# Loading and scaling the mixer's weights inside the convolution, bias per item on VectorE in its last pass, and the first taps loaded apart

## The chip, the cores and the metric

The kernel runs on one core of a Trainium2 chip. The time is device microseconds of one launch. A core has TensorE (PE) for matmuls, with results in PSUM, VectorE (DVE), ScalarE (ACT), GpSimd (POOL) and SyncE (SP), which here only issues transfers. Each engine works through its own instructions in order; semaphores tie them together.

## What is computed

Two layers on x, 64 images of 55 x 55 pixels and 96 channels, f32. The convolution is depthwise: every channel has 25 x 25 taps of which every third row and column counts, without the middle one.

```
m[ix_(arange(0, 25, 3), arange(0, 25, 3))] = 1;  m[12, 12] = 0
lat = depthwise_conv(x, raw_kernel * m, padding='SAME')
x1  = lat * x + bias + x
t   = tokens(x1)                                     # 3025 tokens of 96 per image
h   = relu(bn1(ln(t) @ w1.T));  X = fft(h, over the tokens)
y   = real(ifft(relu(Re(X)*rd - Im(X)*id + rb) + 1j*relu(Im(X)*rd + Re(X)*id + ib)))
t   = t + bn2(y @ w2.T)
out = t + qlinear(relu(qlinear(ln(t), W1, b1)), W2, b2)   # products in 5-bit-exponent, 2-bit-mantissa floats
```

The batch norms' scales and shifts are folded into w1 and w2 on the chip: that is the scaling of the weights, with 1 / sqrt(var + eps) from a Sqrt on ScalarE, a reciprocal and one Newton step on VectorE.

## The kernel before

`build` calls `conv_stage` and then `mixer_stage`; each ends its instruction blocks with all engines meeting.

**The convolution** (L181 to L355) runs 16 passes t: for each of 8 groups of 12 channels (e = t // 2) first the image rows of kind 0, then of kind 1 (k = t % 2). A pass has 36 items n: a channel (n // 3) and a column phase (n % 3). On TensorE an item is three matmuls of x blocks with the channel's band of taps (`toep`, L351) and three transposes of the same blocks by the unit matrix (`unit`, L354), into a pair of PSUM banks; there are four pairs (DEEP = 4), and item m waits until item m - 4 is gated. ScalarE copies the transposed x into `xo` (L297), VectorE then makes (lat + 1) * x there (L328, "the gate"). When all 36 items of a pass are gated, GpSimd adds the bias over the whole pass (`add_bias`, L306): three instructions of 128x3960 for kind 0, two of 128x3300 for kind 1. Of the last pass the second one is VectorE's (`on_dve`). SyncE loads the taps of the next channels, x groups (6 items each) into a ring of three, and stores finished parts of `xo`; a store waits for its part's bias. Before its first matmul TensorE waits for `unit`, then for all 12 channels' taps, then for the first x group. ScalarE's queue issues cbias (the bias on all partitions, 128x96) and then `unit` (114x114), the others are SyncE's.

**The mixer** starts with a block of its own for the weights (L419 to L600): 37 loads (L459), among them the tables fb and ib of the transform (1.8 MB together); VectorE's scaling in steps that wait for each other through w_step (L506 to L558); ScalarE's Sqrt (L575); 36 small matmuls that turn the weights (L584 to L593), and memsets of the mixer's buffers (L563 to L569). After it SyncE issues the first two token loads (L727). The main block then runs over slots g, in which each engine's work for several chunks of tokens stands in a fixed order; VectorE's statistics of the tokens (L1015) and their scaling on GpSimd (L789) come first. In that loop the lines L944 to L960 are the layer norm's root, L969 and L975 the bias and rounding of the feed-forward part, L775 and L779 GpSimd's last additions.

What makes TensorE wait for a gate, and how deep it may run ahead:

```
if m >= DEEP:
    pe.wait_ge(gated, m - DEEP + 1)
```

## Time and profile before

| | |
|---|---|
| three runs, median (lowest, highest) | 4963.41 us (4961.54, 4970.19) |
| profiled execution | 4956.23 us |
| its span, first to last instruction | 4954.4 us |
| mean granted TensorE clock | 0.958 of full |
| busy PE, DVE, ACT, POOL | 4493.3, 3606.6, 3658.7, 2290.2 us |
| DMA | 895.69 MB, mean 181 GB/s |

The profile is of one execution, and the times in it are of that one. Busy time counts an engine's own instructions, not its waits or the issuing of transfers. A row of the timeline has the start, the duration, the engine, the line and operation, the tiles and shapes, how many such instructions follow each other (x), and in brackets how long the engine had been idle and what it waited for last. "SPq" and "ACTq" are the queues of issued transfers.

### The profile page before, as it was taken

To read this page: it belongs to the slowest core of one execution; us is meant where nothing else is said; L and a number is where in the kernel's file an instruction comes from. 1 tells how busy PE (TensorE), PEld (TensorE's weight loads), DVE (VectorE), ACT (ScalarE), POOL (GpSimd) and SP (SyncE) were. 2 spreads that over 40 slices of the span, in tenths; PEclk is the share of its full clock that TensorE was granted. 3 is DMA by queue.
4 is the path that set the end of the run, shared out by engine and by line. 5 is a ranking of instruction groups with operands and counts; after the bars stand their busy time and mean duration, and the time that the engine had idled before them with its cause. 6 is when DMAs were issued, how large, how long until landed. Compare 5 with 4: busy or idle time off the path is not lost.

```text
span 4954.4 us, 170251 instructions
## 1 busy us (share of the span) xinstructions
PE 4493.3 (91%) x64799; PEld 3661.4 (74%) x64799; DVE 3606.6 (73%) x10875; ACT 3658.7 (74%) x7819; POOL 2290.2 (46%) x2603
## 2 busy tenths in 40 slices
PE   8999995699999999999999999999999999999964
PEld 7888885477777777777777777777777777777742
DVE  3444443247888888888888888888888888888865
ACT  3444442377888888888888888888888888888843
POOL 2334432144554545555455555555555555455532
PEclk9999997599999999999999999999999999999975
DMA  6877876366666666666667666666666666666541
GB/s 199 253 235 231 257 227 177 81 173 184 185 182 177 185 176 186 181 185 181 178 179 190 181 185 186 182 186 177 181 179 183 184 182 185 177 180 190 162 102 31
DMA packets 787259, 895.69 MB, mean 181 GB/s; under 512 B 241827, under 2 KB 694880, under 8 KB 774368
## 3 DMA queue, kind: packets, MB, share of 16 engines
q1 hardware_dynamic: 786200, 884.70, 64.1%
q8 instruction: 534, 8.75, 0.8%
q14 instruction: 261, 2.14, 0.1%
q10 hardware_dynamic: 264, 0.10, 0.0%
HBM read 500.05 MB, written 384.61 MB: 179 GB/s over the span
## 4 chain that ended last, share of the span: by engine, by line
PE 57%; DVE 12%; ACT 8%; issue 5%; DMA 0%; DVEq 0%; POOL 0%; POOLq 0%; ACTq 0%
PE ps L1102 13%; PE ps L1089 10%; ACT y L886 7%; PE ps L1121 7%; PE ps L1197 5%; PE ps L1130 4%; PE ps L1146 4%; PE ps L1186 4%; PE ps L1160 4%; PE ps L1173 3%; PE ps L1076 2%; DVE y L969 1%; DVE bn L1022 1%; DVE xn L1007 1%; DVE var L946 1%
## 5 line engine op out<-in xcount | busy, mean ns | idle before, releaser
L763 POOL TENSOR_SCALAR gv<-gv 128x400 f32<-128x400 f32 (+1 forms) x512 | 488.6, 954 | 1673.1 <-DVE xn L1007 1445.3
L1102 PE MATMUL ps<-hid,fa 121*128 121x384 f32 (+1 forms) x2048 | 808.6, 477 | 42.9 <-DVE t L1031 30.6
L351 PE MATMUL cps<-toep,xin 114*128 114x190 f32 (+2 forms) x3456 | 773.1, 338 | 38.7 <-issue 19.8
L886 ACT ACTIVATE y<-ps 128x1089 f16<-128x1089 f32 (+1 forms) x512 | 572.9, 1119 | 314.5 <-PE ps L1186 314.5
L1089 PE MATMUL ps<-w1t,xnt 97*121 97x192 f32 x3200 | 708.9, 332 | 4.8 <-issue 4.2
L297 ACT ACTIVATE xo<-cps 128x180 f32<-128x180 f32 (+3 forms) x576 | 367.6, 638 | 442.4 <-PE cps L354 442.4
L328 DVE SCALAR_TENSOR_TENSOR xo<-cps,xo 128x180 f32<-128x180 f32 (+3 forms) x576 | 362.8, 630 | 450.8 <-ACT xo L297 450.1
L351 PEld LDWEIGHTS cps<-toep,xin 114*128 114x128 f32 x3456 | 529.2, 193 | 102.0 <-issue 25.0
L975 DVE CAST hq<-y 128x1092 fp8e5<-128x1092 f16 (+1 forms) x512 | 537.0, 1049 | 53.1 <-DVE y L969 0.5
L840 ACT ACTIVATE hid<-ps 121x384 f32<-121x384 f32 (+1 forms) x1024 | 438.0, 428 | 174.2 <-PE ps L1089 174.0
L969 DVE TENSOR_SCALAR y<-y,b1q 128x364 f16<-128x364 f16 (+1 forms) x1536 | 476.0, 365 | 107.9 <-ACT y L886 107.9
L306 POOL TENSOR_TENSOR xo<-xo,conv_cbias 128x3960 f32<-128x3960 f32 (+1 forms) x39 | 317.7, 8175 | 506.0 <-DVE xo L328 506.0
L1089 PEld LDWEIGHTS ps<-w1t,xnt 97*121 97x121 f32 x3200 | 530.7, 189 | 23.7 <-issue 5.9
L990 DVE SCALAR_TENSOR_TENSOR spec<-ps,rd,gq 128x400 f32<-128x400 f32 (+1 forms) x512 | 270.8, 529 | 346.7 <-ACT ps L832 342.8
L900 ACT ACTIVATE arow<-ps 128x384 f32<-128x384 f32 (+1 forms) x1024 | 436.3, 426 | 112.3 <-PE ps L1102 91.9
L1076 PE MATMUL ps<-fb,acol 50*64 50x50 f32 x23808 | 469.0, 222 | 34.3 <-issue 13.7
L1121 PE MATMUL ps<-w2t,spec 128*114 128x96 f32 x3968 | 481.2, 264 | 13.1 <-ACT mixed L861 11.1
L1121 PEld LDWEIGHTS ps<-w2t,spec 128*114 128x114 f32 x3968 | 474.1, 182 | 18.7 <-issue 17.2
L789 POOL TENSOR_TENSOR toks<-tok,rstd 121x288 f32<-121x288 f32 (+1 forms) x512 | 354.3, 692 | 257.6 <-DVEq L961 210.7
L775 POOL TENSOR_TENSOR z<-z,b2q 121x288 f16<-121x288 f16 (+1 forms) x512 | 385.5, 753 | 181.3 <-ACT z L869 175.3
L1076 PEld LDWEIGHTS ps<-fb,acol 50*64 50x64 f32 x23808 | 404.9, 135 | 84.9 <-issue 53.1
L1160 PEld LDWEIGHTS ps<-w2q,hq 128*128 128x128 fp8e5 x4800 | 267.9, 100 | 259.4 <-issue 104.6
(110 smaller groups left out, 9654.6 us busy)
## 6 DMA issues: line engine op xcount, KB each, us to landing
a_d<-arow SPq DMA_DIRECT2D x448, 288.0 KB, 5.2
acol<-a_d SPq DMA_DIRECT2D x384, 300.0 KB
xin<-in_items SPq DMA_DIRECT2D x96, 1008.0 KB
g_d<-mixed SPq DMA_DIRECT2D x512, 150.0 KB
tok<-x_d SPq DMA_DIRECT2D x64, 1134.4 KB
out<-o_sb SPq DMA_DIRECT2D x448, 136.1 KB
x_d<-xo SPq DMA_DIRECT2D x48, 990.0 KB, 11.9
grow<-g_d SPq DMA_DIRECT2D x128, 312.0 KB, 10.5
```

Source lines behind the costliest of these rows:

```text
L351: last = nc.tensor.matmul(ps[2 * (m % DEEP)][:, (r0 - o0) * GC:(r1 - o0) * GC], xb, toep[e % 2][0:GP, c, at * GC:(at + r1 - r0) * GC], sta ...
L763: nc.gpsimd.tensor_scalar(v, v, 0.0, None, ALU.max).then_inc(v_cut, 1)
L840: nc.scalar.activation(hid[part][:, 0:s1 - s0, :].rearrange("p j h -> p (j h)"), ps[0:U, WIDE, 0:(s1 - s0) * H], ACT.Relu).then_inc(hid_re ...
L886: nc.scalar.activation(y16[n % 2][:, :, 0:w], ps[:, MIXP:MIXP + FM, 0:w], ACT.Copy).then_inc(y16_ready, 1)
L900: nc.scalar.activation(arow[n % AR][:, s0 - c0:s1 - c0, :].rearrange("p j h -> p (j h)"), ps[0:M, ROW, 0:(s1 - s0) * H], ACT.Copy).then_in ...
L969: last = nc.vector.tensor_scalar(y[:, m, 0:w], y[:, m, 0:w], b1q[:, m:m + 1], 0.0, ALU.add, ALU.max)
L975: nc.vector.tensor_copy(q[:, :, 0:w], y[:, :, 0:w], saturate=False).then_inc(hq_ready, 1)
L1076: last = nc.tensor.matmul(ps[at:at + HALF, r, c0:c0 + K2], acol[HALF * r:HALF * r + K2, p, HALF * (h + 2 * hf):HALF * (h + 2 * hf) + HALF] ...
L1089: last = nc.tensor.matmul(ps[0:U, WIDE, j * H:(j + 1) * H], xnt[n % 2][:, s0 - c0 + j, :], w1t[:, :], start=True, stop=True)
L1102: nc.tensor.matmul(ps[0:M, ROW, 0:(s1 - s0) * H], fa[:, :], hid[part][:, 0:s1 - s0, :].rearrange("p j h -> p (j h)"), start=True, stop=Tru ...
L1121: nc.tensor.matmul(ps[0:HALF + K2, MIXP + a % 2, MIXC + a // 2 * C:MIXC + (a // 2 + 1) * C], wide[:, at:at + HALF + K2], w2t[:, 0, :], sta ...
L1160: last = nc.tensor.matmul(ps[:, DOWNP, C * j:C * (j + 1)], hq[n % 2][:, m, j * U:j * U + 128], w2q[:, m, :], start=(m == 0), stop=(m == FM ...
```

## The change

The small weights, tables fa and ia, and the staging buffers live in their own allocation that is made before the convolution (`weight_buffers`), so they can be filled while it runs. `unit` becomes a view of `ident` (128x128), which ScalarE's queue now issues before cbias. The first two channels' taps are one transfer, awaited before item 0; the other ten follow the first x group and are awaited before item 6. Behind the third x group SyncE issues the 33 loads of the weights. In pass 1 VectorE does the scaling in seven steps between the items, ahead of items 0, 6, 14, 22, 26, 30 and 34, and ScalarE its four Sqrt ahead of item 2. In the last pass GpSimd does nothing; VectorE adds the bias item by item, each after the next item's gate. After the last item TensorE turns the weights and VectorE copies them. In the mixer SyncE issues the tables fb and ib between the first and the second token load, and the memsets stand ahead of VectorE's loop.

```diff
@@ conv_stage
-        unit = sb("unit", [GP, GP])
+        unit = w.ident[0:GP, 0:GP]
...
@@ SyncE
             def load_taps(e):
...
-                sp.dma_start(toep[e % 2][:, :, :],
-                             bands[e].rearrange("p (c t) -> p c t", c=EC)).then_inc(toep_in[e % 2], 16)
+                c0 = 0 if e else CG
+                sp.dma_start(toep[e % 2][:, c0:, :],
+                             bands[e].rearrange("p (c t) -> p c t", c=EC)[:, c0:, :]).then_inc(toep_in[e % 2], 16)
             def store(t, n):
...
-                if on_dve(t, n):
-                    sp.wait_ge(biased[1], 1)
+                if t == PASSES - 1:
+                    sp.wait_ge(biased[1], PER)
...
-            load_taps(0)
+            sp.dma_start(toep[0][:, 0:CG, :],
+                         bands[0].rearrange("p (c t) -> p c t", c=EC)[:, 0:CG, :]).then_inc(toep_first, 16)
             for t in range(PASSES):
...
+                    if n == 0:
+                        load_taps(0)
+                    if n == RING - 1:
+                        load_weights()
@@ ScalarE
+            act.dma_start(w.ident[:, :], p["c_id"]).then_inc(unit_in, 16)
             act.dma_start(cbias[:, :], cb.rearrange("(a c) -> a c", a=1).broadcast_to([128, C])).then_inc(cb_in, 16)
-            act.dma_start(unit[:, :], identity[0:GP, 0:GP]).then_inc(unit_in, 16)
...
+                    if t == 1 and n == 2:
+                        act.wait_ge(w_var, 1)
+                        for v, r in zip(shifted, roots):
+                            last = nc.scalar.activation(r, v, ACT.Sqrt)
+                        last.then_inc(w_root, 1)
@@ GpSimd
-            for t in range(PASSES):
+            for t in range(PASSES - 1):
...
@@ VectorE
+            def shift_variances():
+                dve.wait_ge(w_in, WEIGHTS)
+                for v, n in zip(variances, shifted):
+                    nc.vector.tensor_scalar(n, v, BN_EPS, None, ALU.add)
+                nc.vector.tensor_scalar(w.nrd[:, :], w.rd[:, :], -1.0, None, ALU.mult).then_inc(w_var, 1)
...
+            def bias_item(t, n):
+                c = t // 2 * EC + n // DIL
+                dve.wait_ge(gated, t * PER + n + 1)
+                v = place(t, n)
+                nc.vector.tensor_scalar(v, v, cbias[:, c:c + 1], None, ALU.add).then_inc(biased[1], 1)
             for t in range(PASSES):
...
+                    if t == 1 and n == 0:
+                        shift_variances()
+                    if t == 1 and n == 6:
+                        invert_roots()
+                    if t == 1 and n == 14:
+                        refine_roots()
+                    if t == 1 and n == 22:
+                        scale_weights()
+                    if t == 1 and n == 26:
+                        centre_weights()
+                    if t == 1 and n == 30:
+                        bias_rows()
+                    if t == 1 and n == 34:
+                        round_biases()
...
                     nc.vector.scalar_tensor_tensor(v, lat, 1.0, v, ALU.add, ALU.mult).then_inc(gated, 1)
-            add_bias(nc.vector, PASSES - 1, 1).then_inc(biased[1], 1)
+                    if t == PASSES - 1 and n:
+                        bias_item(t, n - 1)
+            bias_item(PASSES - 1, PER - 1)
+            dve.wait_ge(w_turned, 1)
...
@@ TensorE
-                if k == 0:
+                if k == 0 and e:
                     pe.wait_ge(toep_in[e % 2], 16 * (e // 2 + 1))
...
+                    if m == 0:
+                        pe.wait_ge(toep_first, 16)
+                    if m == STEP:
+                        pe.wait_ge(toep_in[0], 16)
@@ mixer_stage, SyncE
+                if g == FIRST + 1:
+                    sp.dma_start(fb[:, :, :], p["c_fb"]).then_inc(tables_in, 16)
+                    sp.dma_start(ib[:, :, :, :], p["c_ib"]).then_inc(tables_in, 16)
```

VectorE's order at the seam of pass 0 and pass 1 (L328 before and L519 after are the gates; `root`, `var`, `line` and `nrd` are buffers of the scaling), before:

```order
L328 SCALAR_TENSOR_TENSOR xo<-cps,xo 128x18x18 x2
L328 SCALAR_TENSOR_TENSOR xo<-cps,xo 128x10x19
L328 SCALAR_TENSOR_TENSOR xo<-cps,xo 128x10x18 x2
L328 SCALAR_TENSOR_TENSOR xo<-cps,xo 128x10x19
L328 SCALAR_TENSOR_TENSOR xo<-cps,xo 128x10x18 x2
```

and with the change:

```order
L519 SCALAR_TENSOR_TENSOR xo<-cps,xo 128x18x18 x2
L424 TENSOR_SCALAR root<-var 96x2
L424 TENSOR_SCALAR root<-var 96x1
L424 TENSOR_SCALAR line<-line 1x192
L424 TENSOR_SCALAR line<-line 1x96
L425 TENSOR_SCALAR nrd<-rd 128x2
L519 SCALAR_TENSOR_TENSOR xo<-cps,xo 128x10x19
L519 SCALAR_TENSOR_TENSOR xo<-cps,xo 128x10x18 x2
```

Five instructions of the scaling now stand between the last gate of pass 0 and the first of pass 1.

VectorE's order at the end of the convolution (L306 is the bias of the last part, L502 and L506 the first of the weights' block), before:

```order
L328 SCALAR_TENSOR_TENSOR xo<-cps,xo 128x10x19
L328 SCALAR_TENSOR_TENSOR xo<-cps,xo 128x10x18 x2
L306 TENSOR_TENSOR xo<-xo,conv_cbias 128x3300
L186 UNCONDITIONAL_BRANCH
L492 UNCONDITIONAL_BRANCH
L502 MEMSET stage 128x32
L506 TENSOR_SCALAR stage<-stage 96x2
```

and with the change, from the second item's gate of the last pass (the pattern goes on to its end), and behind it the copies:

```order
L519 SCALAR_TENSOR_TENSOR xo<-cps,xo 128x10x18
L491 TENSOR_SCALAR xo<-xo,conv_cbias 128x10x19
L519 SCALAR_TENSOR_TENSOR xo<-cps,xo 128x10x18
L491 TENSOR_SCALAR xo<-xo,conv_cbias 128x10x18
...
L491 TENSOR_SCALAR xo<-xo,conv_cbias 128x10x18 x2
L524 COPY w1t<-cps 96x192
L525 COPY w2t<-cps 128x192
L528 CAST w1q<-cps 96x3x64 x2
L530 CAST w2q<-cps 128x288
```

Gates and bias items now alternate through the last pass, and the one large addition is gone.

## Rows read from the trace of the kernel before

**Rows 1.** Busy time by stretch; columns: length, busy (instructions) per engine, PEclk, DMA share, GB/s.
```profile
18.88:812.50 793.62, 773.81 (x5184) 680.95 (x5184) 362.29 (x575) 367.10 (x575) 307.19 (x38) 0.98 0.75 232
812.50:840.70 28.20, 0.03 (x1) 0.00 (x0) 4.08 (x3) 0.49 (x1) 10.53 (x1) 0.57 0.50 131
840.70:877.15 36.45, 2.17 (x31) 1.79 (x31) 15.29 (x62) 2.11 (x5) 0.00 (x0) 0.50 0.25 71
877.15:895.28 18.13, 0.00 (x1) 0.01 (x1) 6.66 (x40) 0.23 (x1) 0.88 (x2) 0.50 0.63 128
895.28:990.00 94.72, 79.46 (x445) 55.03 (x445) 18.23 (x82) 38.14 (x87) 17.18 (x23) 0.54 0.28 81
990.00:4900.00 3910.00, 3618.45 (x59022) 2911.37 (x59015) 3179.80 (x10061) 3233.72 (x7125) 1940.82 (x2518) 0.98 0.65 176
```

**Rows 2.** Timeline of the start: ScalarE's queue, and TensorE at items 0, 2 and 3.
```profile
0.71 0.41 ACTq L285 DMA_DIRECT2D conv_cbias<-in_L_conv_bias  x1
1.15 0.58 ACTq L286 DMA_DIRECT2D unit<-in_c_id  x1
18.89 1.51 PE L351 MATMUL cps<-toep,xin 114*128 114x342 f32 x2 [18.89 <-DMA unit<-in_c_id]
...
24.75 0.75 PE L351 MATMUL cps<-toep,xin 114*128 114x342 f32 x2
...
26.31 0.75 PE L351 MATMUL cps<-toep,xin 114*128 114x342 f32 x2
```

**Rows 3.** Busy time by stretch, while the first transfers run.
```profile
2.00:17.00 15.00, 0.00 (x0) 0.00 (x0) 0.00 (x0) 1.04 (x1) 0.00 (x0) 1.00 0.97 288
```

**Rows 4.** Timeline of the convolution's end.
```profile
813.09 0.48 DVE L328 SCALAR_TENSOR_TENSOR xo<-cps,xo 128x180 f32<-128x180 f32 x1 [0.58 <-ACT xo L297]
813.61 3.60 DVE L306 TENSOR_TENSOR xo<-xo,conv_cbias 128x3300 f32<-128x3300 f32 x1
813.65 10.53 POOL L306 TENSOR_TENSOR xo<-xo,conv_cbias 128x3300 f32<-128x3300 f32 x1 [12.31 <-DVE xo L328]
824.21 6.12 SPq L254 DMA_DIRECT2D x_d<-xo  x4
```

**Rows 5.** Timeline of the weights: VectorE's first step, SyncE after it; the stretch of refinement.
```profile
859.60 0.22 DVE L506 TENSOR_SCALAR stage<-stage 96x2 f32<-96x2 f32 x2 [18.73 <-DMA idg<-in_L_attn_i]
...
863.52:866.58 3.06, 0.00 (x0) 0.00 (x0) 2.87 (x17) 0.00 (x0) 0.00 (x0) 0.50 0.00 0
...
877.15 1.07 SPq L727 DMA_DIRECT2D tok<-x_d  x2
```

**Rows 6.** Timeline: GpSimd's bias in pass 1, 2 and 15, and a gate in 15.
```profile
79.47 25.84 POOL L306 TENSOR_TENSOR xo<-xo,conv_cbias 128x3960 f32<-128x3960 f32 x3 [79.05 <-DVE xo L328]
117.54 7.18 POOL L306 TENSOR_TENSOR xo<-xo,conv_cbias 128x3300 f32<-128x3300 f32 x1 [12.23 <-DVE xo L328]
...
775.50 25.84 POOL L306 TENSOR_TENSOR xo<-xo,conv_cbias 128x3960 f32<-128x3960 f32 x3 [48.99 <-DVE xo L328]
...
776.55 0.49 DVE L328 SCALAR_TENSOR_TENSOR xo<-cps,xo 128x180 f32<-128x180 f32 x1 [0.48 <-ACT xo L297]
```

**Rows 7.** Timeline of the mixer: VectorE beside GpSimd; last, L947's durations (min/median/max).
```profile
1389.11 0.66 POOL L789 TENSOR_TENSOR toks<-tok,rstd 121x288 f32<-121x288 f32 x1
1389.73 0.74 POOL L775 TENSOR_TENSOR z<-z,b2q 121x288 f16<-121x288 f16 x1
1389.43 0.45 DVE L969 TENSOR_SCALAR y<-y,b1q 128x364 f16<-128x364 f16 x1 [0.51 <-ACT y L886]
1389.80 0.78 DVE L969 TENSOR_SCALAR y<-y,b1q 128x364 f16<-128x364 f16 x1
...
4673.26 0.81 POOL L779 TENSOR_TENSOR o_sb<-t,z 121x288 f32<-121x288 f32 x1
4673.50 0.60 DVE L947 TENSOR_SCALAR mean<-mean 121x25 f32<-121x25 f32 x1
...
L947 DVE TENSOR_SCALAR mean<-mean x69: 178/190/637, 892.0 to 4880.1; 121x50 f32<-121x50 f32 x59, 121x25 f32<-121x25 f32 x10
```

More of the change, by code:

```diff
@@ L1 @@
 from contextlib import ExitStack
+from dataclasses import dataclass
 import numpy as np
@@ L208, in conv_stage @@
         biased = [sem("biased_pool"), sem("biased_dve")]
+        toep_first = sem("toep_first")
+        w_in = sem("w_in")
+        w_var = sem("w_var")
+        w_root = sem("w_root")
+        w_step = sem("w_step")
+        w_scaled = sem("w_scaled")
+        w_turned = sem("w_turned")
+        w_clear = sem("w_clear")
         PASSES = 2 * E
@@ L310, in _ @@
             pool.wait_ge(cb_in, 16)
-            for t in range(PASSES):
+            for t in range(PASSES - 1):
+                e, k = t // 2, t % 2
                 pool.wait_ge(gated, PER * (t + 1))
-                for n in range(len(parts(t % 2))):
-                    if not on_dve(t, n):
-                        add_bias(nc.gpsimd, t, n).then_inc(biased[0], 1)
+                cbe = cbias[:, e * EC:(e + 1) * EC]
+                for r0, r1 in parts(k):
+                    v = xo[k][e % 2][:, r0:r1, :, :].rearrange("p r x c -> p (r x) c")
+                    nc.gpsimd.tensor_tensor(v, v, cbe.unsqueeze(1).broadcast_to([128, (r1 - r0) * R, EC]),
+                                            ALU.add).then_inc(biased[0], 1)
@@ new lines, in invert_roots, with refine_roots @@
+            def invert_roots():
+                dve.wait_ge(w_root, 1)
+                for v, r in zip(variances, roots):
+                    last = nc.vector.reciprocal(v, r)
+                then(last)
+            def refine_roots():
+                for v, r in zip(variances, roots):
+                    last = nc.vector.tensor_tensor(r, v, v, ALU.mult)
+                then(last)
+                for r, n in zip(roots, shifted):
+                    last = nc.vector.tensor_tensor(r, r, n, ALU.mult)
+                then(last)
+                for r in roots:
+                    last = nc.vector.tensor_scalar(r, r, -0.5, 1.5, ALU.mult, ALU.add)
+                then(last)
+                for v, r in zip(variances, roots):
+                    last = nc.vector.tensor_tensor(v, v, r, ALU.mult)
+                then(last)
@@ new lines, in scale_weights @@
+            def scale_weights():
+                nc.vector.tensor_tensor(gam1[:, :], gam1[:, :], var1[:, :], ALU.mult)
+                nc.vector.tensor_tensor(gam2[:, :], gam2[:, :], var2[:, :], ALU.mult)
+                nc.vector.tensor_tensor(rows1[0], rows1[0], rows1[3], ALU.mult)
+                then(nc.vector.tensor_tensor(rows2[0], rows2[0], rows2[3], ALU.mult))
+                for a in range(2):
+                    nc.vector.tensor_scalar(w1n[:, a, :], w1n[:, a, :], gam1[:, a:a + 1], None, ALU.mult)
+                then(nc.vector.tensor_scalar(w2n[:, :], w2n[:, :], gam2[:, :], None, ALU.mult))
@@ L353, in _, with mixer_stage @@
                                                 start=(i == 0), stop=(i == BLK - 1))
-                        last = nc.tensor.transpose(ps[2 * (m % DEEP) + 1][:, q * GP:(q + 1) * GP], xb, unit[:, :])
+                        last = nc.tensor.transpose(ps[2 * (m % DEEP) + 1][:, q * GP:(q + 1) * GP], xb, unit)
                     last.then_inc(lat_done, 1)
-def mixer_stage(nc, x1, p, a_d, g_d, out):
+            pe.wait_ge(gated, PER * PASSES)
+            pe.wait_ge(w_in, WEIGHTS)
+            pe.wait_ge(w_scaled, 1)
+            pe.wait_ge(w_clear, 1)
+            ident = w.ident
+            for a in range(2):
+                nc.tensor.transpose(ps[0][0:C, a * HH:(a + 1) * HH], w1n[:, a, :], ident[0:HH, 0:HH])
+                nc.tensor.transpose(ps[1][:, a * C:(a + 1) * C], w2n[:, a * 128:(a + 1) * 128], ident[0:C, 0:C])
+            for m in range(FM):
+                nc.tensor.transpose(ps[3][:, m * C:(m + 1) * C], m2[:, m * 128:(m + 1) * 128], ident[0:C, 0:C])
+            for m in range(FM):
+                for r in range(2):
+                    for h in range(2):
+                        last = nc.tensor.matmul(ps[4 + r][64 * h:64 * h + 64, 64 * m:64 * m + 64],
+                                                m1[64 * r:64 * r + 64, C * m + 64 * h:C * m + 64 * h + 64],
+                                                ident[64 * r:64 * r + 64, 64 * r:64 * r + 64],
+                                                start=True, stop=True)
+            last.then_inc(w_turned, 1)
+def mixer_stage(nc, x1, p, w, a_d, g_d, out):
     with ExitStack() as ctx:
@@ L1251, in build @@
     g_d = nc.dram_tensor("g_d", [B, S, M, C], F32).ap()
-    conv_stage(nc, p["items"], p["bands"], p["cb"], p["c_id"], x1)
-    mixer_stage(nc, x1, p, a_d, g_d, out)
+    with ExitStack() as ctx:
+        w = weight_buffers(nc, ctx)
+        conv_stage(nc, p["items"], p["bands"], p["cb"], p, w, x1)
+        mixer_stage(nc, x1, p, w, a_d, g_d, out)
 def kernel(**inputs):
```

326 lines of the change are left out of this document (134 added, 192 removed).

## The prediction

> **What bounds the kernel now.** I read the stages first (the busy time of each engine by stretch), then the timeline at the three seams between them, and last what VectorE and GpSimd do to each other. The convolution holds TensorE 97.5% busy, 773.8 of 793.6 us, and the mixer 93% [rows 1]; both are bound by TensorE. So the change can win only at the seams, and loses wherever it makes TensorE wait. The seams are long. TensorE does nothing for 18.9 us at the start, and the row names the transfer of `unit` as the last thing it waited for [rows 2]. After its last matmul at 812.5 us come 28.2 us in which the last pass's bias is added and stored, then 36.4 us of loading and scaling weights, with 2.2 us of matmuls in them, then 18.1 us of first tokens [rows 1].
>
> In what follows pass 1 is items 36 to 71 (kind 1 of the first eight channels), pass 15 the last one. All times are of the old trace; I add the shifts at the end.
>
> **Start: a gain of 11.1 us.** `unit` has its 0.6 us issue at 1.15 us behind cbias, and is awaited until 18.89 [rows 2]. `ident` now goes ahead of cbias and has 128 rows. TensorE then needs the first two channels' taps (128 x 2 x 342 x 4 B = 0.35 MB), `ident` (0.07 MB) and the first x group (1.05 MB), 1.47 MB in all. Between 2 and 17 us the transfers moved 288 GB/s [rows 3], so that is 5.1 us from 2 us on; with some 0.7 us for landing, TensorE starts at 7.8 us. Bounds: at 16 us if `ident` still drags (it was the small transfer, not the big ones, that came last), at 6.5 if the head start counts fully. Its first six items take about 12 us, since the first two of them cost 5.86 us together (18.89 to 24.75) and the others 1.56 each [rows 2]; item 6 at 19.9 needs the other ten channels and the second x group, 4.3 MB, there at about 17.7. So no second wait. The 33 loads issued behind the third x group cost TensorE nothing if they take SyncE the 0.5 us each that they take now (36.4 us hold 37 of them and the scaling, and the last landed at 859.60 [rows 1, 5]): SyncE is free at about 21 us, and x group 3 is needed only at 38.6.
>
> **The weights' stretch: a gain of 36.4 us.** It runs from 840.70 to 877.15, where the first tokens are loaded [rows 1, 5]. All of it goes: the loads lie under the convolution, the 36 small matmuls and four copies under the last stores, and the memsets, now ahead of the mixer's loop, under the 10 us in which the first tokens land. The tables fb and ib (1.8 MB) now go between the first and second token loads and delay the second by 7 us; its statistics are wanted only at slot 6, so nothing waits.
>
> **Pass 1: a loss of 19.8 us.** What is inserted is small: of the seven steps the longest, the Newton refinement, took 3.06 us [rows 5]. Items come every 1.075 us (776.55 to 813.09 is 34 of them), VectorE works 0.49 us in each [rows 4, 6], and with four pairs of banks TensorE can go on for 2.1 us when a gate is late (three items less the 1.05 us from an item's last matmul to the end of its gate). So by length alone the steps cost 3.06 - 2.1 and a little for the reciprocals and the Sqrt with its table: 1.5 us.
>
> But pass 1 is also where GpSimd adds pass 0's bias: three instructions of 8.6 us back to back, 79.47 to 105.3 [rows 6], and the first step stands on VectorE exactly there. What two engines do when they meet is in rows 7. A TENSOR_SCALAR on y issued at 1389.43, inside a GpSimd instruction that ended at 1389.77, took 0.45 us and not 0.30; the next, inside GpSimd's next one (1389.73 to 1390.47), took 0.78 and ended 0.11 us after it. On f32 it is the same: `mean` takes 0.18 to 0.19 us as a rule and took 0.60 when GpSimd began at 4673.26 and ended at 4674.07. And two-input additions shut each other out: of GpSimd's bias, 7.18 us alone, the last one took 10.53, 3.35 more, when VectorE had begun its own 3.60 us 0.04 us earlier [rows 4, 6, 7]. So a VectorE instruction of these kinds waits for the whole GpSimd instruction, then one gets through, then GpSimd's next one goes. The gates themselves (one input from PSUM) ran through GpSimd's 8.6 us at 0.49 [rows 6].
>
> The Trainium skill has this as a rule that speaks against the change: SBUF — State Buffer, "Who interferes with whom", says that VectorE in a two-port mode, or with two inputs in SBUF, and GpSimd take one port pair for a whole instruction and the other "fully blocks"; VectorE: DVE Perf Modes, "Mode 2×_2P", counts any single-input f32 instruction in SBUF with an even outermost dimension, so the strided ones too. By the rule each meeting costs up to 8.6 us; by the lengths alone the whole change would give 4907. The rows bear the rule out, though only for GpSimd instructions of up to 1.3 us.
>
> Of the first step's five instructions (96x2, 96x1, 1x192, 1x96, 128x2) the first three take 0.6 us and are through about when GpSimd starts, 0.15 us after the last gate. The fourth waits for the first 8.6 us, the fifth for the second. Item 36's gate ends at 97.5 and not 79.9, 17.6 later; less 2.1 that is 15.5 of TensorE. Having stood so long it comes back slow: at the start it lost 5.86 - 2 x 1.55 = 2.8 us [rows 2]; the granted clock shows no fall there, so I take the loss from the durations. With the 1.5 from above: 19.8. Bounds: 1.5 (none blocked) and 28.5 (three blocked). The later steps find GpSimd done.
>
> **Pass 15: a loss of 12.7 us, where 10.3 were to be gained.** The intent: last gate at 813.57, last bias item 0.3 later, stores issued at 813.9 and not 824.21 [rows 4]. But GpSimd adds pass 14's bias from 775.50 to 801.3 [rows 6]. Bias item 0 follows gate 1, at 777, and waits until 784.1; then gate 2; bias 1 waits for the second instruction, bias 2 for the third, until 801.9 with handovers. Gate 4 ends at 802.7, and TensorE starts item 8 there, not at 782.4 (812.5 less 28 items): 20.3 late, and 2.8 for coming back slow. From there VectorE's 0.8 us an item fit into 1.075. The last gate ends at 836.6, the last bias at 836.9: 12.7 after the 824.2 of now. Pass 14's stores, issued as pass 15 advances, end near 838 and fill the lead of the last ones.
>
> **Sum:** -11.1 - 36.4 + 19.8 + 12.7 = -15.0 us. The profiled execution took 4956.2, so 4941.2; it lies 7.2 below the median of the three runs, and the change's runs should lie as far above theirs: 4963.4 - 15.0 = **4948.4**. Below 0.2%, 10 us, a measurement of this kernel can't tell a change from none.
>
> **Rivals.**
> - *No blocking*: the strided 10x19 pieces and the tiny ones never shut out GpSimd; no row shows such shapes. -11.1 - 36.4 + 1.5 - 10.3 = -56.3: 4907. Against: rows 7. Chance 0.13.
> - *Blocked only in pass 1*: -11.1 - 36.4 + 19.8 - 10.3 = -38.0: 4925. Chance 0.10. *Only bias items and two-input steps*: then the refinement at item 14 meets the second and third GpSimd instruction, 2.7 + 8.7 + 3.1 - 2.1 + 2.8 = 15.2 in pass 1: 4944. Chance 0.08.
> - *Three blocked in pass 1* (the third instruction comes too late as well), 8.7 more: 4957. Chance 0.16. It hangs on a tenth of a microsecond.
> - *The scaling's loads hold SyncE*: 33 issues stall behind 5 MB, and x group 3 comes 5 to 10 us late: near 4955. For it: SyncE issued 37 in 18 us only with an emptier queue. Chance 0.05.
> - *Slower: TensorE's clock stays down.* Its granted clock was 0.54 over the mixer's first 95 us although it was busy 84% of them [rows 1]. If after each of the two stalls it stays at the lower level (1.2 instead of 2.4 GHz) to the end of the pass, 60 items cost 0.95 us more each, 57 less the 5.6 counted: 4999. It decides from 16 more slow items on. Against: at the start it was back after 5.9 us, and the convolution is denser than the mixer's start. Chance 0.08.
>
> The forecast keeps 0.40. **Range:** 4905 to 4966 takes in all but the slow clock and the margins of the first rival. The likeliest case's own range is 4940 to 4958. **Chances:** faster by over 0.2% (below 4953.5) 0.13 + 0.10 + 0.07 + 0.29 of the forecast + 0.03 = 0.62; within 0.2% 0.30; slower 0.08.
>
> **What would show it.** TensorE's first matmul at 7.8 us; two TENSOR_SCALARs of the scaling near 8.6 us long at the start of pass 1, three of bias items as long in pass 15; GpSimd's instructions near 8.6 us still, not longer; TensorE idle for 15 and 20 us there, with its clock down after; stores at 837 less 11.1 plus 19.8, 845.6; first tokens issued at 862.2 instead of 877.15. I am wrong if these VectorE instructions run at 0.2 to 0.3 us beside GpSimd (then 4907), or if the clock row of the passes stays near 0.5.

## The result, and the profile after

The changed kernel took 4926.41 us (median of 4 runs, 4920.29 to 4936.07) against 4964.98 of the kernel before on the same chip: a ratio of 0.9927, 95% interval 0.9908 to 0.9947. The prediction was 4948.4 with a range of 4905 to 4966. A second, larger comparison (below, ten runs of each kernel and a shared set of 21) gave 0.9959, 0.9942 to 0.9976: 16 to 20 us less (by medians and by ratio), not 38. Both are faster by more than 0.2%; single executions of either kernel spread over 20 to 40 us, so the terms of the sum have to be read from profiles, gate by gate.

The same stretches as in [rows 1], of the profile after (length, busy per engine, clock, DMA share, GB/s):

```profile
0.00:9.87 9.87, 0.00 (x0) 0.03 (x1) 0.09 (x1) 1.28 (x1) 0.19 (x4) 1.00 0.81 221
9.87:71.80 61.93, 59.23 (x330) 47.82 (x331) 26.62 (x35) 27.35 (x36) 0.00 (x0) 1.00 0.65 181
71.80:129.50 57.70, 41.23 (x321) 39.73 (x318) 43.87 (x86) 20.40 (x42) 25.69 (x4) 0.85 0.58 176
129.50:789.40 659.90, 638.22 (x4222) 557.47 (x4223) 299.00 (x468) 303.43 (x468) 255.43 (x32) 0.98 0.77 237
789.40:850.95 61.55, 43.75 (x316) 41.62 (x314) 50.45 (x72) 18.24 (x36) 25.76 (x3) 0.81 0.52 164
850.95:868.00 17.05, 1.29 (x31) 1.04 (x31) 2.12 (x8) 0.00 (x0) 0.00 (x0) 0.58 0.77 200
```

Passes 1 and 15, the third and the fifth row, have TensorE busy for 41 of 58 and 44 of 62 us; the stretch between them is as dense as the old convolution (97%). Last gate to first tokens, the sixth row, is 17 us where it was 63.6 (813.57 to 877.15, [rows 4, 5]).

The start (timeline, SyncE's queue, and TensorE's first instruction), answering to [rows 2]:

```profile
9.87 1.48 PE L554 MATMUL cps<-toep,xin 114*128 114x342 f32 x2 [9.87 <-DMA xin<-in_items]
...
7.22 12.05 SPq L315 DMA_DIRECT2D m<-in_L_ffn_W  x2
...
34.20 0.58 SPq L354 DMA_DIRECT2D xin<-in_items  x1
```

TensorE starts 9.0 us earlier, now behind the first x group and not behind the identity. SyncE then stands 12 us in two of the 33 loads and issues x group 3 at 34.2 us.

Pass 1 (timeline of VectorE, GpSimd and ScalarE), answering to [rows 6]:

```profile
72.74 0.21 DVE L424 TENSOR_SCALAR root<-var 96x2 f32<-96x2 f32 x2
72.97 8.72 DVE L424 TENSOR_SCALAR line<-line 1x192 f32<-1x192 f32 x2
81.70 8.42 DVE L425 TENSOR_SCALAR nrd<-rd 128x2 f32<-128x2 f32 x1
90.03 0.87 DVE L519 SCALAR_TENSOR_TENSOR xo<-cps,xo 128x190 f32<-128x190 f32 x2
...
72.98 25.68 POOL L408 TENSOR_TENSOR xo<-xo,conv_cbias 128x3960 f32<-128x3960 f32 x3 [72.55 <-DVE xo L519]
...
90.15 0.30 ACT L389 ACTIVATE root<-root 96x2 f32<-96x2 f32 x2 [14.90 <-DVE nrd L425]
```

Three of the five small instructions run in 0.14 to 0.26 us each, the fourth and the fifth take 8.5 and 8.4 us, one for each GpSimd instruction of 8.56 us. The gate behind them comes at 90.03.

Pass 15 (timeline of VectorE):

```profile
791.05 0.49 DVE L519 SCALAR_TENSOR_TENSOR xo<-cps,xo 128x180 f32<-128x180 f32 x1 [0.41 <-ACT xo L395]
791.44 7.33 DVE L491 TENSOR_SCALAR xo<-xo,conv_cbias 128x190 f32<-128x190 f32 x1
798.68 0.47 DVE L519 SCALAR_TENSOR_TENSOR xo<-cps,xo 128x180 f32<-128x180 f32 x1
799.06 8.30 DVE L491 TENSOR_SCALAR xo<-xo,conv_cbias 128x180 f32<-128x180 f32 x1
807.27 0.49 DVE L519 SCALAR_TENSOR_TENSOR xo<-cps,xo 128x190 f32<-128x190 f32 x1
807.67 8.27 DVE L491 TENSOR_SCALAR xo<-xo,conv_cbias 128x180 f32<-128x180 f32 x1
```

Three bias items stand for three GpSimd instructions (789.99 to 815.75), with one gate between each two. What TensorE pays is in the view of waits, up to 851 us (total, times, longest):

```profile
PE cps L554 <- DVE xo L519: 32.1, 5, 15.0
PE cps L554 <- issue: 22.8, 7, 4.5
PE cps L554 <- DMA xin<-in_items: 12.6, 3, 9.9
```

32.1 us behind VectorE's gates; there was no such row before. The row "issue" was there too (19.8 us, seven times).

The end (timeline of SyncE's queue and VectorE's copies), answering to [rows 4, 5]:

```profile
851.58 6.25 SPq L309 DMA_DIRECT2D x_d<-xo  x4
867.98 0.31 SPq L750 DMA_DIRECT2D tok<-x_d  x1
...
852.37 0.35 DVE L524 COPY w1t<-cps 96x192 f32<-96x192 f32 x1 [0.81 <-PE cps L572]
852.64 0.34 DVE L525 COPY w2t<-cps 128x192 f32<-128x192 f32 x1
852.91 0.61 DVE L528 CAST w1q<-cps 96x192 fp8e5<-96x192 f32 x2
853.44 0.44 DVE L530 CAST w2q<-cps 128x288 fp8e5<-128x288 f32 x1
```

The stores follow the last gate by 0.6 us (it was 10.6), and the weights' copies lie under them.

### The profile page after: what moved, and what is told of

The parts are those of the page before. It is cut to its first block, busy times and chain, and to the rows that moved or that the text cites. A ratio compares the mean times of both kernels' runs of the same rounds, so it can differ in the third digit from the quotient of the medians.

```text
span 4927.0 us, 170278 instructions
## 1 busy us (share of the span) xinstructions
PE 4496.8 (91%) x64799; PEld 3663.0 (74%) x64799; DVE 3649.5 (74%) x10911; ACT 3659.7 (74%) x7819; POOL 2281.3 (46%) x2602
## 4 chain that ended last, share of the span: by engine, by line
PE 57%; DVE 12%; ACT 8%; issue 4%; DMA 0%; DVEq 0%; POOL 0%; POOLq 0%; SPq 0%; ACTq 0%
PE ps L1138 13%; PE ps L1125 10%; ACT y L912 7%; PE ps L1157 7%; PE ps L1233 5%; PE ps L1166 4%; PE ps L1182 4%; PE ps L1222 4%; PE ps L1196 4%; PE ps L1209 3%; PE ps L1112 2%; DVE y L995 1%; DVE bn L1048 1%; DVE xn L1033 1%; DVE var L972 1%
## 5 line engine op out<-in xcount | busy, mean ns | idle before, releaser
L554 PE MATMUL cps<-toep,xin 114*128 114x190 f32 (+2 forms) x3456 | 780.7, 340 | 67.5 <-DVE xo L519 32.1
L519 DVE SCALAR_TENSOR_TENSOR xo<-cps,xo 128x180 f32<-128x180 f32 (+3 forms) x576 | 361.5, 629 | 429.6 <-ACT xo L395 429.0
L408 POOL TENSOR_TENSOR xo<-xo,conv_cbias 128x3960 f32<-128x3960 f32 (+1 forms) x38 | 306.9, 8104 | 508.4 <-DVE xo L519 508.4
```

The lines of the kernel that those rows point to most:

```text
L554: last = nc.tensor.matmul(ps[2 * (m % DEEP)][:, (r0 - o0) * GC:(r1 - o0) * GC], xb, toep[e % 2][0:GP, c, at * GC:(at + r1 - r0) * GC], sta ...
```

## The experiments

One table for all profiles. "Pass 0" is the time of its last gate but one; the passes are counted from last gate but one to last gate but one, "seam" from there to the first token load, "mixer" from that load to the end of the span. The first three rows are the kernel before, three times.

| profile | first matmul | pass 0 | pass 1 | passes 2 to 14 | pass 15 | seam | tokens at | mixer |
|---|---|---|---|---|---|---|---|---|
| before | 18.9 | 77.8 | 38.6 | 657.4 | 38.7 | 64.6 | 877.2 | 4077.3 |
| r1_before_again | 20.4 | 78.6 | 38.7 | 663.8 | 38.7 | 64.5 | 884.3 | 4077.3 |
| r12_before_third | 18.7 | 76.9 | 38.7 | 668.2 | 38.7 | 64.6 | 887.0 | 4061.5 |
| after | 9.9 | 71.3 | 57.1 | 660.0 | 61.5 | 18.1 | 868.0 | 4059.1 |
| r2_after_again | 9.9 | 73.8 | 56.9 | 662.7 | 60.1 | 18.1 | 871.6 | 4074.5 |
| r3_bias_undone | 11.0 | 74.3 | 57.5 | 656.9 | 38.7 | 28.2 | 855.6 | 4060.8 |
| r4_scaling_late | 9.8 | 71.8 | 38.8 | 661.5 | 60.0 | 18.2 | 850.3 | 4061.9 |
| r5_both_gone | 9.8 | 70.6 | 39.4 | 662.6 | 39.3 | 18.2 | 830.1 | 4078.9 |
| r6_bias_on_scalare | 9.8 | 72.8 | 38.8 | 664.4 | 38.7 | 18.4 | 833.1 | 4062.3 |
| r7_loads_late | 11.0 | 70.1 | 57.5 | 660.7 | 61.4 | 17.8 | 867.5 | 4069.8 |
| r8_taps_whole | 14.7 | 73.1 | 57.1 | 662.1 | 60.5 | 17.7 | 870.6 | 4065.2 |
| r9_all_three | 11.5 | 70.7 | 38.8 | 662.4 | 39.2 | 18.2 | 829.4 | 4046.6 |
| r10_one_port_form | 9.6 | 71.3 | 38.9 | 661.4 | 38.7 | 18.2 | 828.4 | 4065.1 |
| r11_gpsimd_in_pieces | 9.8 | 71.5 | 38.9 | 667.2 | 46.1 | 18.2 | 841.9 | 4061.5 |

Passes 1 and 15 and the seam repeat to within some tenths (pass 15 with its stalls: 60.0 to 61.5); passes 2 to 14 and the mixer move by 10 and 30 us whatever the edit.

**The two kernels again** (r1 and r2, no edit).

> The kernel before, once more, for the length of its mixer. From the first token load to the end it took 4077.3 us in the profile of before, the change's 4059.1, though nothing of the change lies there but two table loads. Theory A (chance of one execution: what instruction fetches and transfers cost varies): this profile's mixer lies anywhere between 4055 and 4080. Theory B (something of the layout in memory or code makes the mixer of the change shorter): again 4072 to 4080. Median 4965 either way.

> The changed kernel, once more. Theory A: its mixer takes anything from 4055 to 4080 us. Theory B: again 4055 to 4064. The convolution's parts should repeat: first matmul at 9.9 us, two VectorE instructions of about 8.5 us at the start of pass 1, three of 7 to 8.5 us in the last pass, last gate at 851.

Measured: 4961.38 us for the kernel before, ratio 1.0007 (0.9994 to 1.0020); 4941.41 us for the changed one, 0.9959 (0.9942 to 0.9976). The stalls come back in the second profile to within 0.02 us: 8.54 and 8.42 in pass 1, 7.31, 8.29 and 8.27 in pass 15 (what follows them in pass 15 was 1.4 us shorter). What doesn't come back is part of the first result's 38 us. The mixers took 4077.3 us again in the kernel before, and 4074.5 in the changed one, outside the range of theory B.

**The last pass's bias put back** (r3).

```diff
-                if t == PASSES - 1:
-                    sp.wait_ge(biased[1], PER)
+                if t == PASSES - 1 and n == 1:
+                    sp.wait_ge(biased[1], 1)
@@ GpSimd
-            for t in range(PASSES - 1):
+            for t in range(PASSES):
...
-                for r0, r1 in parts(k):
+                for r0, r1 in parts(k)[:1 if t == PASSES - 1 else None]:
@@ VectorE, after the loop
-            bias_item(PASSES - 1, PER - 1)
+            dve.wait_ge(gated, PER * PASSES)
...
+            nc.vector.tensor_tensor(v, v, cbe, ALU.add).then_inc(biased[1], 1)
```

> The change, with the last pass's bias as it was (GpSimd the first part, VectorE the second in one instruction after the last gate). Theory (bias items wait for GpSimd's whole instructions): the three long VectorE instructions of the last pass go, TensorE runs through it, the last gate comes 22.9 us earlier (828), GpSimd's last bias ends 10.6 us after it, and the stores are issued at 838.7 instead of 851.6: 13 us faster, 4913. Rival (the last pass is slow for another reason, such as the stores or the clock): the last gate stays near 850 and the time rises by the 10 us of GpSimd's bias, to 4936.

Measured: 4933.67 us, 0.9954 (0.9935 to 0.9973). Pass 15 is back at 38.7 us and the seam 10.1 longer: from pass 14 to the tokens 66.9 us where the changed kernel takes 79.6 (78.2 in its second profile). The bias moved to VectorE item by item costs 11 to 13 us net. The last gate at 828.1 to 828.5 decides against the rival. The time doesn't: 4933.67 is 20 us above the 4913 expected, which was counted from the first result's 4926.41, and beside the repeat's 4941.41 in the same comparison it is 8 less, with intervals that overlap (0.9959 and 0.9954). The gain of r3 rests on the profiles. Its timeline at the end shows the old picture of [rows 4], 3.60 beside 10.54 us:

```profile
828.57 3.60 DVE L523 TENSOR_TENSOR xo<-xo,conv_cbias 128x3300 f32<-128x3300 f32 x1
...
828.61 10.54 POOL L408 TENSOR_TENSOR xo<-xo,conv_cbias 128x3300 f32<-128x3300 f32 x1 [12.31 <-DVE xo L519]
```

**The scaling moved to where GpSimd is idle** (r4): the seven steps stand ahead of items 26 and 32 of pass 1, 26, 30 and 33 of pass 3, 27 and 31 of pass 5, and ScalarE's Sqrt ahead of item 28 of pass 1.

```diff
-                    if t == 1 and n == 0:
+                    if t == 1 and n == 26:
                         shift_variances()
-                    if t == 1 and n == 6:
+                    if t == 1 and n == 32:
                         invert_roots()
-                    if t == 1 and n == 14:
+                    if t == 3 and n == 26:
                         refine_roots()
...
```

> The change, with the seven steps of the scaling moved to the last third of passes 1, 3 and 5, where GpSimd has finished the bias of the pass before. Theory (the first step waits for GpSimd): no VectorE instruction of the scaling takes over 2 us, pass 1 costs at most 1.5 us instead of 18.4, 17 us faster: 4909. Rival (the steps cost by their own length and by the Sqrt's table load): each costs the same wherever it stands, and the time stays at 4926 within 4.

Measured: 4918.21 us, 0.9917 (0.9896 to 0.9937), 9 us above the 4909 expected and 23 below the repeat of the changed kernel in the same comparison. Pass 1 takes 38.8 us. The same instructions, grouped by line and shape (mean ns behind the busy us), and then TensorE's row in the view of waits:

```profile
L424 DVE TENSOR_SCALAR line<-line 1x96 f32<-1x96 f32 x1 | 0.2, 198 | 0.0
L425 DVE TENSOR_SCALAR nrd<-rd 128x2 f32<-128x2 f32 x1 | 0.2, 169 | 0.0
```

```profile
PE cps L554 <- DVE xo L519: 17.1, 4, 6.1
```

The 1x96 takes 198 ns and not 8.5 us, the 128x2 169 ns and not 8.42 us. All that is left of pass 1's 18.3 us is 0.1, with the reciprocals and the Sqrt still in that pass, so it wasn't the Sqrt either; the steps moved to pass 3 cost 0.5 us (39.2 where 38.7 were before), those in pass 5 nothing. TensorE's wait behind VectorE's gates falls from 32.1 to 17.1 us; that rest is pass 15's.

**Both stalls gone** (r5), with the last pass's bias a channel at a time from item 25 on, so that it still ends with the last gate.

```diff
...
-                nc.vector.tensor_scalar(v, v, cbias[:, c:c + 1], None, ALU.add).then_inc(biased[1], 1)
+            def bias_channel(c):
+                t = PASSES - 1
+                dve.wait_ge(gated, t * PER + DIL * (c + 1))
+                v = xo[1][t // 2 % 2][:, :, :, c]
+                b = t // 2 * EC + c
+                nc.vector.tensor_scalar(v, v, cbias[:, b:b + 1], None, ALU.add).then_inc(biased[1], 1)
...
+                    if t == PASSES - 1 and n >= LATE and (n - LATE) % 2 == 0 and (n - LATE) // 2 < 5:
+                        bias_channel(2 * ((n - LATE) // 2))
+                        bias_channel(2 * ((n - LATE) // 2) + 1)
```

> Scaling steps moved out of GpSimd's bias as in the run before, and the last pass's bias added a channel at a time on VectorE from item 25 of the pass on, when GpSimd's three bias instructions are over. Theory (a VectorE instruction with its operands in SBUF waits for GpSimd's whole instruction; nothing else of the change costs TensorE time in these passes): pass 1 and pass 15 both take about 38.7 us from their second to their last gate, the last gate comes at 810 to 811 us, the stores about a microsecond later, the first tokens at 828. No VectorE instruction over 2 us in either pass. Time 22 to 23 us under the run with the scaling late alone. Rival (VectorE's own load, gate and bias together, is what delays pass 15): the last gate stays near 825 to 833, since the same additions are now pressed into the last ten items.

Measured: 4894.97 us, 0.9881 (0.9856 to 0.9905). Passes 1 and 15 take 39.4 and 39.3 us, the last gate comes at 812.3, the tokens at 830.1 (some 2 us later than expected), and no VectorE instruction of the pass is long:

```profile
L493 DVE TENSOR_SCALAR xo<-xo,conv_cbias 128x550 f32<-128x550 f32 x12 | 8.2, 733 | 0.0
```

The rival falls: 8.2 us of additions pressed into the last third of the pass cost TensorE 0.6 us. So the amount of VectorE's work is not what delayed pass 15.

**The bias items on ScalarE** (r6; scaling late too), in the middle of GpSimd's bias.

```diff
@@ ScalarE
+            def bias_item(t, n):
+                c = t // 2 * EC + n // DIL
+                act.wait_ge(gated, t * PER + n + 1)
+                v = xo[t % 2][t // 2 % 2][:, :, n % DIL::DIL, n // DIL]
+                nc.scalar.activation(v, v, ACT.Identity, bias=cbias[:, c:c + 1]).then_inc(biased[1], 1)
...
+                    if t == PASSES - 1 and n > 1:
+                        bias_item(t, n - 2)
```

> Scaling late as before, and the last pass's bias items put on ScalarE, item by item two items behind the copy, so that they stand in the whole of GpSimd's bias instructions. Theory (only VectorE and GpSimd shut each other out): bias items of 0.3 to 0.5 us on ScalarE also between 770 and 800 us, GpSimd's three at 8.6 us, pass 15 in 38.7 us, last gate at 810 to 811, as in the run with both stalls gone. Rival (whoever works in SBUF beside GpSimd waits): three ScalarE items of 8 us, the last gate at about 833 as with the scaling late alone.

Measured: 4908.57 us, 0.9904 (0.9884 to 0.9925). Groups of pass 15:

```profile
L384 ACT ACTIVATE xo<-xo,conv_cbias 128x180 f32<-128x180 f32 x24 | 14.3, 600 | 0.0
...
L420 POOL TENSOR_TENSOR xo<-xo,conv_cbias 128x3960 f32<-128x3960 f32 x3 | 25.9, 8693 | 48.7 <-DVE xo L531 48.7
```

0.60 us each, somewhat over the 0.3 to 0.5 expected, and none blocked; pass 15 takes 38.7 us. (The last gate came at 815.7 and not 810 to 811: pass 0 and passes 2 to 14 were longer in this execution than in r5.) The same addition in the same place costs TensorE nothing on ScalarE, and waits on VectorE.

**The loads behind the sixth x group** (r7) and **the taps in one piece again** (r8).

```diff
-                    if n == RING - 1:
+                    if n == 5:
                         load_weights()
```

```diff
-            sp.dma_start(toep[0][:, 0:CG, :],
-                         bands[0].rearrange("p (c t) -> p c t", c=EC)[:, 0:CG, :]).then_inc(toep_first, 16)
+            load_taps(0)
...
-                c0 = 0 if e else CG
-                sp.dma_start(toep[e % 2][:, c0:, :],
-                             bands[e].rearrange("p (c t) -> p c t", c=EC)[:, c0:, :]).then_inc(toep_in[e % 2], 16)
+                sp.dma_start(toep[e % 2][:, :, :],
+                             bands[e].rearrange("p (c t) -> p c t", c=EC)).then_inc(toep_in[e % 2], 16)
```

> The changed kernel with the 33 loads of the weights issued by SyncE behind the sixth x group and not behind the third. Theory (SyncE stands in the loads while its queue is full, and the fourth and fifth x groups come late for that): TensorE's wait for the items before item 18 and 24 goes, the gate of item 24 comes at about 49.5 and not 52.6 us, the gate of item 35 at 68 to 68.5 and not 71.3; 3 us less in all, unless the same blocking comes later in the pass. Rival (the x groups are late because the other taps, 1.75 MB, now go between the first and the second x group): gates as in the changed kernel.

> The changed kernel with all twelve channels' taps in one transfer ahead of the first x group, as before the change; the identity is still the first on ScalarE's queue. Theory (the first matmul waits for bytes: taps and first x group at 250 to 290 GB/s): 1.75 MB more stand ahead of the first x group, the first matmul at 15 to 17 us and not 9.9, and all gates of pass 0 later by about as much, less what later waits take up. Rival (the start was lost to the late identity alone, and the order of the taps is free): first matmul at 10 to 11 us.

Measured: 4930.23 us, 0.9952 (0.9936 to 0.9969), and 4938.85 us, 0.9965 (0.9945 to 0.9984). In r7 x group 3 is issued at 23.51 us, the two loads that stood 12 us take 0.96, and all 33 take 15.9 us (43.13 to 59.01) where the changed kernel needs 29.2 (5.05 to 34.20):

```profile
23.51 0.32 SPq L354 DMA_DIRECT2D xin<-in_items  x1
...
45.58 0.96 SPq L315 DMA_DIRECT2D m<-in_L_ffn_W  x2
```

Between 35 and 72 us TensorE no longer waits for an x group; the changed kernel shows this row there:

```profile
PE cps L554 <- DMA xin<-in_items: 2.7, 2, 1.4
```

But my figures for r7 missed: the gate of item 24 came at 53.0 and not 49.5 (52.6 in the changed kernel), that of item 35 at 70.1 and not 68 to 68.5, since the first matmul was 1.1 us late and the first items slower. By the last gate but one of pass 0, r7 stands at 70.1 (and r9, below, at 70.7) against 70.6 to 74.3 in the eight kernels with early loads and taps apart (mean 72.2). Counted from the first gate to that of the pass's last item, r7 and r9 both take 55.7 us and those eight 57.4 to 60.5. So the direction is shown; the size, 2 us in absolute time, is not well measured, because both kernels with late loads also started 1 to 2 us later than most, and whether that belongs to the edit is open (r3, with early loads, started at 11.0 too). In r8 the first matmul comes at 14.72 and not 9.87 (15 to 17 were expected):

```profile
14.72 1.48 PE L547 MATMUL cps<-toep,xin 114*128 114x342 f32 x2 [14.72 <-DMA xin<-in_items]
```

That splits the start: 4.2 us came with the identity put first (18.9 to 14.7), 4.9 with the taps apart. At the end of pass 0, though, r8 stands at 73.1, within the spread of the kernels that started 4.9 us sooner, and it too has no wait for x groups between 35 and 72 us. With the loads issued early, the head start of the taps is spent again waiting for x groups 3 and 4.

**All three put right** (r9): r5 with the loads behind the sixth x group.

> Scaling late, last pass's bias by channel from item 25 on, and the 33 loads behind the sixth x group. Theory (the three losses are independent): against the run with both stalls gone, which had its item-35 gate 57.4 us after the first and in which the fourth and fifth x groups came late, 3 to 4 us less by the end of pass 0; item 35's gate 54.2 to 54.5 us after the first; last gate at 808 to 810, first tokens at 826 to 827, about 4892 us. Rival (the loads' 12 us of standing only moves to a place where it hurts as much): last gate at 812 or more.

Measured: 4891.03 us, 0.9867 (0.9846 to 0.9889), the fastest version, 70 us below the kernel before in its comparison; it can't be told from r5 (0.9856 to 0.9905). Item 35's gate came 55.7 us after the first gate and not 54.2 to 54.5 (57.4 in r5), and the last at 811.6, between the two expectations, with a first matmul 1.7 us later than r5's. The loads' order is worth 1.7 us from the first gate on against r5, 3 against the mean of the eight, and by the end of the convolution less than 1 against r5.

**Another form of the same instruction** (r10), scaling late.

```diff
-                nc.vector.tensor_scalar(v, v, cbias[:, c:c + 1], None, ALU.add).then_inc(biased[1], 1)
+                if n < LATE:
+                    nc.vector.tensor_scalar(v, v, cbias[:, c:c + 1], 0.0, ALU.add, ALU.add,
+                                            accum_out=sums[:, n:n + 1]).then_inc(biased[1], 1)
+                else:
+                    nc.vector.tensor_scalar(v, v, cbias[:, c:c + 1], None, ALU.add).then_inc(biased[1], 1)
```

> Scaling late; the last pass's first 25 bias items use the form of the same VectorE instruction that also writes a sum (here into a spare column), which the Trainium skill (SBUF — State Buffer, Who interferes with whom) leaves out of the forms that take the port pair shared with GpSimd. Theory (it is the two-port mode that shuts the engines out): these items take 0.5 to 0.7 us and not 0.38, none takes 8 us, also between 775 and 802 us; GpSimd's three stay at 8.6 us; pass 15 takes 39 to 41 us and the last gate comes at 811 to 815. Rival (any VectorE instruction that reads and writes SBUF waits for GpSimd): three items of 8 us as before, last gate at 833 or later.

Measured: 4908.20 us, 0.9891 (0.9867 to 0.9915). Groups of pass 15 on VectorE and GpSimd:

```profile
L494 DVE TENSOR_SCALAR_CACHE_REDUCE xo<-xo,conv_cbias 128x180 f32<-128x180 f32 x16 | 8.8, 551 | 0.0
L494 DVE DVE_READ_ACCUMULATOR xo<-xo,conv_cbias 128x1 f32 x25 | 2.2, 89 | 0.0
L497 DVE TENSOR_SCALAR xo<-xo,conv_cbias 128x180 f32<-128x180 f32 x8 | 3.0, 390 | 0.0
...
L410 POOL TENSOR_TENSOR xo<-xo,conv_cbias 128x3960 f32<-128x3960 f32 x3 | 25.9, 8695 | 48.8 <-DVE xo L525 48.8
```

The form that also writes a sum is slower by itself, 551 against 390 ns, and runs beside GpSimd's 8.7 us as if it weren't there: pass 15 takes 38.7 us. So reading and writing SBUF is not what shuts VectorE out; the faster form of the instruction is. This is what the Trainium skill says (SBUF — State Buffer, "Who interferes with whom": `tensor_scalar` contends, "not the form that also writes out its accumulator"), and the trace agrees. Which ports an instruction takes no row here shows, only which form waits.

**GpSimd's work in 18 pieces** (r11), scaling late. A piece is 128x660 elements (the expectation gives its shape wrongly).

```diff
+                    d = 1 if t == PASSES - 2 else r1 - r0
+                    for q in range(r0, r1, d):
...
-                    nc.gpsimd.tensor_tensor(v, v, cbe.unsqueeze(1).broadcast_to([128, (r1 - r0) * R, EC]),
-                                            ALU.add).then_inc(biased[0], 1)
+                        last = nc.gpsimd.tensor_tensor(v, v, cbe.unsqueeze(1).broadcast_to([128, d * R, EC]),
+                                                       ALU.add)
+                    last.then_inc(biased[0], 1)
```

> Scaling late; GpSimd adds pass 14's bias in 18 pieces of one row (128x220 elements each x 12 channels' share, a sixth of a part) and not in 3. The work is the same. Theory (a waiting VectorE instruction gets in at every end of a GpSimd instruction, and only there): the bias items of the last pass take 1.3 to 1.6 us each while GpSimd works, 13 to 18 of them, and no TensorE idle time of 15 us; the items come every 1.9 to 2.1 us there, so pass 15 takes 50 to 53 us and not 61, last gate at 822 to 826. Rival (the length of the lock does not matter, only the total of GpSimd's work): last gate at 833 as with the scaling late alone.

Measured: 4899.30 us, 0.9880 (0.9858 to 0.9903). Timelines of pass 15 (GpSimd, then three of VectorE's rounds):

```profile
779.21 29.63 POOL L410 TENSOR_TENSOR xo<-xo,conv_cbias 128x660 f32<-128x660 f32 x18 [48.03 <-DVE xo L522]
...
783.01 1.34 DVE L494 TENSOR_SCALAR xo<-xo,conv_cbias 128x180 f32<-128x180 f32 x1
784.25 0.49 DVE L522 SCALAR_TENSOR_TENSOR xo<-cps,xo 128x180 f32<-128x180 f32 x1
784.64 1.35 DVE L494 TENSOR_SCALAR xo<-xo,conv_cbias 128x190 f32<-128x190 f32 x1
```

One bias item gets in for each piece: they come every 1.65 us (29.63 over 18), and TensorE's longest wait for a gate is 0.4 us. Pass 15 takes 46.1 us, better than the 50 to 53 I had expected, because I had added the bias item's own time to the piece's. A piece alone would take 1.44 us by division (25.84 over 18, an estimate), so a round is only some 0.2 us longer, with a bias item of 0.39 in it. (The last gate fell into my window, 824.7, only because passes 2 to 14 took 667 us in this execution.) The rival falls: with the same work for GpSimd the loss of pass 15 sinks from 21 (r4) to 7.4 us.

**The kernel before, a third profile** (r12, no edit), for the mixer.

> The kernel before, a third profiled execution. In question is the mixer, from the first token load to the end: 4077.3 us in both profiles of the kernel before, 4046.6 to 4078.9 in eleven of kernels with the change. Theory (chance from execution to execution): anything from 4055 to 4072 here. Rival (the change makes the mixer some 10 us shorter): 4075 to 4080 again. The convolution: first tokens at 877 to 884.

Measured: 4958.22 us, 1.0008 (0.9991 to 1.0024). The mixer took 4061.5 us, so the kernel before has the short one too, and 4077 is no property of it. The tokens came at 887.0, outside my window, for passes 2 to 14 took 668 us.

## Why the prediction was right, and where it wasn't

Against the means of the three profiles before and the two of the changed kernel:

| step | forecast | measured |
|---|---|---|
| start, to the end of pass 0 | -11.1 | -5.2 |
| pass 1 | +19.8 | +18.3 |
| pass 15, bias, stores, weights | +12.7 - 36.4 = -23.7 | +22.1 - 46.5 = -24.4 |
| passes 2 to 14 | 0 | -1.7, chance |
| to the first tokens | -15.0 | -13.0 |
| mixer | 0 | -5.2, chance or not |
| sum | -15.0 | -18.2 |

- **Pass 1: right in mechanism and size.** Two of five small instructions stood 8.5 and 8.4 us, the first three got through, and TensorE's longest wait was 15.0 us (15.5 forecast). Moving the steps (r4) took all but 0.1 us away. The rival with three blocked did not come true, but by 0.01 us: the pair with VectorE's third instruction stands at 72.97, GpSimd's start at 72.98. The margin was 0.01 to 0.03 us in all five profiles with this order, so it repeats, but nothing in the forecast's 0.6 us for three instructions against 0.15 to GpSimd's start could tell it: that two and not three were blocked was luck. The rival "only bias items and two-input steps" falls, since it was the 1x96 and the 128x2 that stood. That no row of before had shows such shapes, 1x96 or 128x2, didn't matter.
- **Pass 15: right.** Three bias items blocked, 22.1 us of delay against 20.3 + 2.8, undone by r3 (11 to 13 us net, 12.7 forecast), by another engine (r6), by another form (r10) and by another time (r5). The rivals "no blocking" and "blocked only in pass 1" fall with it.
- **Coming back slow: the size near, its row not of the same kind.** The 2.8 us after each stall were read from the start, where the granted clock was 1.00. After the stalls it was lower (pass 1 of the changed kernel):

```profile
90.00:95.00 5.00, 4.43 (x19) 4.26 (x20) 2.29 (x6) 2.19 (x7) 5.00 (x2) 0.50 0.00 2
95.00:100.00 5.00, 5.00 (x39) 4.85 (x39) 3.95 (x8) 2.12 (x5) 3.66 (x1) 0.90 0.71 206
```

  That is 58 matmuls in 10 us where the next 5 us hold 45, so about 3 us lost by my estimate, and 3 to 4 by the same count behind the stall in pass 15 (19 and 35, last section). That 2.8 was near is luck in part.
- **Weights' stretch: right.** From the last gate to the tokens 46.5 us went, 46.7 forecast (36.4 and 10.3).
- **Start: the wrong step.** "That is 5.1 us from 2 us on" took the transfers in order of issue and at 288 GB/s. At 9.87 us the engines had moved 221 GB/s x 9.87 us = 2.2 MB, 0.7 MB more than the 1.47 MB that were waited for: other transfers moved beside these. 2.1 us of the gain were missing; how they divide between that and the 0.7 us for landing, for which the forecast showed no row, stays open. The rest is the small rival, "the scaling's loads hold SyncE", which I gave 0.05 and which came true beside the forecast: "0.5 us each" was read where the queue was empty; behind three x groups two of them took 12.05 us (11.6 to 13.6 in the nine kernels with early loads), and x group 3, for which SyncE was to be free at 21, was issued at 34.2. Its price was smaller than the 6 to 7 us I gave: from item 17 to 34 these kernels took 3 to 5 us more than the 26.5 of the kernel before (29.7 in the changed one). It takes both, early loads and the head start: r7 has no such wait without the first, r8 none without the second.
- **The slow clock** stayed a rival: the clock was at 0.50 after both stalls and back at full in the same pass (rows above and last section).
- **The median.** My 4948.4 missed the first result's 4926.41 by 22 us, the repeat's 4941.41 by 7. Three mixers of before and two of after differ by 5 us in the mean, with a spread from 4047 to 4079 over all fourteen. Whether the change shortens the mixer by a few us stays open; the 18.2 us between the first two profiles are little more than what one kernel shows by itself (15.8 us between three profiles of before, 15.4 between two of the changed one).
- **The sum: partly luck.** -15.0 forecast and -18.2 in the profiles are near because misses cancel: the start gave 5.9 us less than forecast, pass 1 and pass 15 were 2.2 us better, and the rest is passes 2 to 14 and the mixer, 6.9 us of what executions differ by. To the first tokens, where the change acts, it is -13.0 for -15.0.

## What to carry to other kernels

Before small VectorE work is slipped under another engine's time, look at what GpSimd runs there: the price is not the length of the inserted instruction but of the GpSimd instruction it meets, once for each. In this kernel the same work cost TensorE nothing, or 0.6 us, when it stood behind GpSimd's instructions, on ScalarE, or in a form that is slower by itself; or cut GpSimd's instruction, so that each meeting is short. And read an issue's price where its queue is as full as it will be: loads put ahead of a stream's next transfer hold that up.
